# A graph layer on one core: attention in products of 128x128, the message sum in products of 512 columns, one-hots made from SBUF

## What is computed

```python
ea  = edge_attr @ w_e + b_e                       # 131072 x 256
msg = relu(x[src] + ea)
agg = segment_sum(msg, dst, num_segments=8192)
t   = x + agg
h_local = bn(relu(t @ w1 + b1) @ w2 + b2 + x)

hd = x.reshape(256, 32, 256)                      # 256 groups of 32 nodes
q, k, v = split(hd @ in_w.T + in_b)               # 4 heads of 64
attn = softmax(q k^T / 8)                         # 32 x 32 per group and head
h_attn = bn((attn v) @ out_w.T + out_b + x)

out = h_local + h_attn
out = bn(out + relu(out @ m_w1 + m_b1) @ m_w2 + m_b2)
y   = layernorm(x + out)
```

## Time and profile before

| | |
|---|---|
| median of 3 runs | 1954.65 us (1941.84 to 1976.45) |
| the profiled execution | 1932.73 us, its span 1930.9 us |
| TensorE matmul busy | 1567.5 us, 81% |
| TensorE weight load busy | 1182.9 us, 61% |
| VectorE busy | 761.7 us, 39% |
| ScalarE busy | 817.6 us, 42% |
| GpSimd busy | 970.3 us, 50% |
| mean granted clock of TensorE | 0.865 |

### The profile page before, as it was taken

The page is one execution under the profiler, slowest core; times in us unless marked ns, Lnnn a source line. Parts: engine busy times, 40 slices in busy tenths (PEclk is TensorE's granted clock), DMA queues, the critical chain, the costliest instruction groups (busy, mean ns, idle before and its releaser), DMA issues.

```text
span 1930.9 us, 30540 instructions
## 1 busy us (share of the span) xinstructions
PE 1567.5 (81%) x11522; PEld 1182.9 (61%) x11522; DVE 761.7 (39%) x1465; ACT 817.6 (42%) x1729; POOL 970.3 (50%) x1032
## 2 busy tenths in 40 slices
PE   5878888887878888887777887888888787888787
PEld 3556566565656666665666665666666566666566
DVE  4334433343333433433433443433433333433343
ACT  2334434453334444444444443444444444444452
POOL 6554534555445555554455554645555455555430
PEclk6779888898888988888888887989888888888899
DMA  8545533444333434433443433433433334433321
GB/s 292 166 164 178 183 109 99 118 125 121 96 93 113 131 116 118 122 111 93 118 120 110 123 105 104 133 113 113 125 104 114 111 117 114 121 106 107 108 86 34
DMA packets 107385, 233.42 MB, mean 121 GB/s; under 512 B 21731, under 2 KB 46563, under 8 KB 105189
## 3 DMA queue, kind: packets, MB, share of 16 engines
q0 software_dynamic: 49152, 134.28, 24.1%
q1 hardware_dynamic: 56640, 93.87, 14.9%
q10 hardware_dynamic: 1444, 3.30, 0.5%
HBM read 206.20 MB, written 25.17 MB: 120 GB/s over the span
## 4 chain that ended last, share of the span: by engine, by line
PE 66%; issue 15%; another core or an unknown queue 9%; ACT 4%; DVE 4%; DMA 0%; POOL 0%; DVEq 0%; ACTq 0%
PE bank L670 26%; PE bank L716 15%; PE bank L698 14%; PE bank L800 5%; PE bank L786 2%; DVE ml L527 2%; ACT mh L316 2%; PE bank L870 1%; PE bank L704 1%; ACT bank L310 1%; PE bank L725 1%; PE bank L809 1%; ACT h L327 0%; DVE onehot L543 0%
## 5 line engine op out<-in xcount | busy, mean ns | idle before, releaser
L280 POOL DMA_INDIRECT xg<-xb_dram,srcs x864 | 817.2, 946 | 755.5 <-ACT bank L310 520.0
L527 DVE SCALAR_TENSOR_TENSOR ml<-bank,mh 128x512 fp32r<-128x512 f32 x512 | 349.2, 688 | 963.3 <-ACT mh L316 781.4
L316 ACT ACTIVATE mh<-bank 128x512 fp32r<-128x512 f32 x512 | 300.4, 601 | 978.1 <-PE bank L698 551.7
L716 PE MATMUL bank<-mh,onehot 128*128 128x256 f32 x1024 | 346.9, 358 | 123.1 <-DVE ml L527 103.7
L716 PEld LDWEIGHTS bank<-mh,onehot 128*128 128x128 f32 x1024 | 210.7, 206 | 264.5 <-issue 221.6
L310 ACT COPY bank<-xg 128x512 f32<-128x512 f32 x512 | 307.5, 601 | 69.8 <-DVE ml L527 32.8
L698 PE MATMUL bank<-we,ea 64*128 64x256 f32 x2048 | 334.9, 449 | 0.5 <-issue 0.5
L716 PE MATMUL bank<-ml,onehot 128*128 128x256 f32 x1024 | 288.8, 301 | 0.0
L698 PEld LDWEIGHTS bank<-we,ea 64*128 64x128 f32 x2048 | 200.7, 211 | 99.8 <-issue 71.4
L280 POOL DMA_INDIRECT xg<-in_x_dram,srcs x160 | 152.1, 950 | 143.9 <-ACT bank L310 98.8
L716 PEld LDWEIGHTS bank<-ml,onehot 128*128 128x128 f32 x1024 | 215.3, 210 | 1.6
(11 more groups left out here) (100 smaller groups left out, 1319.5 us busy)
## 6 DMA issues: line engine op xcount, KB each, us to landing
ea<-in_ea_dram SPq DMA_DIRECT2D x128, 256.0 KB
xg<-xb_dram,srcs POOLq DMA_INDIRECT x864
xT<-in_xT_dram SPq DMA_DIRECT2D x32, 256.0 KB
aggT<-in_xT_dram SPq DMA_DIRECT2D x32, 256.0 KB
xrow<-in_x_dram SPq DMA_DIRECT2D x8, 1024.0 KB
xb_dram<-xrow SPq DMA_DIRECT2D x8, 1024.0 KB
oT_dram<-oT SPq DMA_DIRECT2D x32, 256.0 KB
xn<-in_x_dram SPq DMA_DIRECT2D x32, 256.0 KB
```

The source lines that it names most:

```text
L280: pool.indirect_dma_start(xg[:, q % NX, n * C:(n + 1) * C], None, t["x"] if q < XB_PAIR else k.xb_dram[:, :], bass.IndirectOffsetOnAxis(k. ...
L316: nc.scalar.activation(mh[:, q % 4, :], EA[q % 3][:, :], ACT.Relu).then_inc(s_mh, 1)
L527: nc.vector.scalar_tensor_tensor(ml[:, q % 4, :], EA[q % 3][:, :], 0.0, mh[:, q % 4, :].bitcast(fp32), ALU.max, ALU.subtract).then_inc(s_m ...
L716: ins = nc.tensor.matmul(G[n % 2][:, 0:C], onehot[:, n % 2, 2 * j + two, :], half[:, q % 4, two * C:(two + 1) * C], start=j == 0 and two = ...
```

## The change

The scores become 8 calls in place of 32 in each iteration: a half of 128 nodes by itself, so that the scores of nodes of different groups are made too and not used. The two banks of the scores become one tensor `both` of 1024 columns, and VectorE reads the four diagonal blocks of 32x32 out of it: maximum, subtraction and the transpose are four instructions each, one per 32 partitions over 8 x 32 elements. `probT` is 128x128 per head with zeros outside the diagonal blocks, set once at the start. The product with v is 8 calls with v as the stationary operand, and its result is already transposed: the copy at p = 14 (L355), the transposes (L809) and their waits are gone, and the copy for the node network moves from p = 16 to p = 14.

`mh` and `ml` become one tile `msg` with high and low side by side; one float32r matmul of 512 columns takes the place of two of 256, and high and low sums arrive in the two halves of the bank `G`. They are added after the group: ScalarE copies the high half to SBUF as before, and VectorE adds the low half onto it (`join_agg`, p = 3, 7, 11, 15) before TensorE's transpose. Since the bank is full, the row of 0 to 127 and the bias row are read from SBUF, and the copies into the bank at the start are gone; the wait for the bias row moves to the first `add_be`.

```diff
-        k.EA, k.G, k.X = k.bank[0:3], k.bank[3:5], k.bank[5:8]
+        k.EA, k.G = k.bank[0:3], k.bank[3:5]
+        k.both = ctx.enter_context(nc.psum_tensor("both", [P, 1024], fp32))
+        k.X = [k.both[:, 0:512], k.bank[5], k.both[:, 512:1024]]
...
-        k.mh, k.ml = sb("mh", [P, 4, 2 * C], f32r), sb("ml", [P, 4, 2 * C], f32r)
+        k.msg = sb("msg", [P, 4, 2, 2 * C], f32r)
...
-                nc.scalar.copy(k.agg[:, :], G[n % 2][:, 0:C]).then_inc(s_agg, 1)
+                nc.scalar.copy(k.agg[:, :], G[n % 2][:, 0:C]).then_inc(s_high, 1)
...
                 if p == 14:
                     act.wait_ge(s_av, i + 1)
-                    if i >= 1:
-                        act.wait_ge(s_oT, i)
-                    nc.scalar.copy(k.on[:, :], X[1][:, :]).then_inc(s_on, 1)
-                if p == PI:
-                    act.wait_ge(s_oT, i + 1)
                     if i >= 2:
...
+            step_of(nc.vector.memset(k.probT[:, :, :], 0.0))
...
                 nc.vector.tensor_tensor(
                     onehot[:, n % 2, :, :],
-                    G[n % 2][:, 2 * P:3 * P].unsqueeze(1).to_broadcast([P, TG, P]),
+                    k.iota[:, :].unsqueeze(1).to_broadcast([P, TG, P]),
...
+            def join_agg(n):
+                dve.wait_ge(s_high, n + 1)
+                nc.vector.tensor_tensor(k.agg[:, :], G[n % 2][:, C:2 * C], k.agg[:, :], ALU.add
+                                        ).then_inc(s_agg, 1)
...
+                quarter = [slice(n * NPG, (n + 1) * NPG) for n in range(P // NPG)]
+                scores = k.both[:, :].rearrange("p (h n) -> p h n", n=P)
...
+                    for g in quarter:
+                        ins = nc.vector.tensor_reduce(k.mx[g, :], scores[g, :, g], AX.X, ALU.max)
...
+                    for g in quarter:
                         ins = nc.vector.tensor_tensor(
+                            k.dif[g, :, :], scores[g, :, g],
+                            k.mx[g, :].unsqueeze(2).to_broadcast([NPG, 2 * H, NPG]), ALU.subtract)
...
+                    for g in quarter:
+                        ins = nc.vector.transpose(k.probT[g, :, g], k.prob[g, :, :])
...
                 for two in range(2):
-                    for half in (mh, ml):
-                        ins = nc.tensor.matmul(G[n % 2][:, 0:C], onehot[:, n % 2, 2 * j + two, :],
-                                               half[:, q % 4, two * C:(two + 1) * C],
+                    ins = nc.tensor.matmul(G[n % 2][:, :], onehot[:, n % 2, 2 * j + two, :],
+                                           msg[:, q % 4, :, two * C:(two + 1) * C],
...
+                            ins = nc.tensor.matmul(X[2 * (h % 2)][:, col:col + P],
+                                                   k.qT[at:at + DH, c, row], k.kT[at:at + DH, c, row],
+                                                   start=True, stop=True)
...
+                            at, col = DH * (h % 2), h // 2 * NB + b * P
+                            ins = nc.tensor.matmul(X[1][at:at + DH, col:col + P],
+                                                   k.vn[:, b, h * DH:(h + 1) * DH],
+                                                   k.probT[:, H * (h % 2) + 2 * b + h // 2, :],
+                                                   start=True, stop=True)
```

More of the change, by code:

```diff
@@ L167, in program @@
         s_out = [sem(f"s_out_stored_{n}") for n in range(2)]
-        s_go = sem("s_general_go")
+        s_go, s_high = sem("s_general_go"), sem("s_high_sum_copied")
         g = General(sem)
@@ L534, in add_be @@
                 dve.wait_ge(s_xrow[m % 2], 16 * (m // 2 + 1))
+                if n == 0:
+                    dve.wait_ge(s_ber, 16)
                 part = k.xrow[:, m % 2, :, half * P:(half + 1) * P]
                 nc.vector.tensor_tensor(
-                    part, G[half][:, 3 * P:4 * P].unsqueeze(1).to_broadcast([P, XB_ROWS, P]), part,
+                    part, k.be_rows[:, half * P:(half + 1) * P].unsqueeze(1).to_broadcast([P, XB_ROWS, P]), part,
                     ALU.add).then_inc(s_xadd, 1)
@@ L647, in _ @@
                     low(slot - 2)
+                if slot % PG == 3 and 1 <= slot // PG <= NG:
+                    join_agg(slot // PG - 1)
                 if slot % PG == 1:
@@ L714, in sum_pair @@
                 for two in range(2):
-                    for half in (mh, ml):
-                        ins = nc.tensor.matmul(G[n % 2][:, 0:C], onehot[:, n % 2, 2 * j + two, :],
-                                               half[:, q % 4, two * C:(two + 1) * C],
-                                               start=j == 0 and two == 0 and half is mh,
-                                               stop=j == PG - 1 and two == 1 and half is ml)
+                    ins = nc.tensor.matmul(G[n % 2][:, :], onehot[:, n % 2, 2 * j + two, :],
+                                           msg[:, q % 4, :, two * C:(two + 1) * C],
+                                           start=j == 0 and two == 0,
+                                           stop=j == PG - 1 and two == 1)
                 ins.then_inc(s_seg, 1)
@@ L780, in attention @@
                     for b in range(2):
+                        row = slice(b * P, (b + 1) * P)
                         for h in range(H):
                             at, c = DH * (h % 2), h // 2
-                            col = (2 * b + c) * NPG
-                            for n in range(4):
-                                o = b * P + n * NPG
-                                ins = nc.tensor.matmul(
-                                    X[2 * (h % 2)][n * NPG:(n + 1) * NPG, col:col + NPG],
-                                    k.qT[at:at + DH, c, o:o + NPG], k.kT[at:at + DH, c, o:o + NPG],
-                                    start=True, stop=True)
+                            col = (2 * b + c) * P
+                            ins = nc.tensor.matmul(X[2 * (h % 2)][:, col:col + P],
+                                                   k.qT[at:at + DH, c, row], k.kT[at:at + DH, c, row],
+                                                   start=True, stop=True)
                     ins.then_inc(s_sc, 1)
@@ L797, in attention @@
                         for h in range(H):
-                            for n in range(4):
-                                r = slice(n * NPG, (n + 1) * NPG)
-                                ins = nc.tensor.matmul(
-                                    X[1][r, b * C + h * DH:b * C + (h + 1) * DH],
-                                    k.probT[r, H * (h % 2) + 2 * b + h // 2, :],
-                                    k.vn[r, b, h * DH:(h + 1) * DH], start=True, stop=True)
-                    ins.then_inc(s_av, 1)
-                if p == 15:
-                    pe.wait_ge(s_on, i + 1)
-                    for c in range(CC):
-                        for b in range(2):
-                            ins = nc.tensor.transpose(
-                                X[1][:, c * NB + b * P:c * NB + (b + 1) * P],
-                                k.on[:, b * C + c * P:b * C + (c + 1) * P], ident[:, :])
-                    ins.then_inc(s_oT, 1)
+                            at, col = DH * (h % 2), h // 2 * NB + b * P
[3 more added lines that the diff above has]
+                                                   start=True, stop=True)
+                    ins.then_inc(s_av, 1)
             def node(j, step):
```

40 lines of the change are left out of this document (8 added, 32 removed).

## The result

| | before | changed |
|---|---|---|
| median of 4 runs each, on one chip | 1950.05 us (1941.84 to 1976.45) | 1787.34 us (1775.59 to 1790.50) |
| ratio, 95% interval | | 0.9167 [0.9102, 0.9233] |
| span of the profiled execution | 1930.9 us | 1783.1 us |
| TensorE busy, idle | 1567.5, 363.4 us | 1446.6, 336.5 us |
| mean granted clock | 0.865 | 0.90 |

What follows compares the result with a forecast made beforehand. TensorE was taken as the bound, its small attention products limited by how fast instructions reach the array. −300 − 93 − 11 + 64 = −340 us on 1930.9 gave 1591, stated as 1600 us; range 1420 to 1720.

Steps and rivals of the forecast that it cites:

- Rival C: TensorE stalls per instruction anywhere, so gaps move and waiting shrinks only to the remaining matmuls' share, 0.63: 1740 us; chance 0.13.
- Attention, −300 us: TensorE's scores, product with v and transposes: 390 us removed, 32 × 2.8 us added for the larger matmuls.
- The clock, −93 us: TensorE's slow clock behind the small products' gaps goes with them: 2.9 us an iteration.
- The sum, −11 us: Message sum on TensorE: two matmuls of 512 columns for four of 256 save 0.022 us a pair.
- rival D: The 512-column float32r message sum runs at float32's pace of two passes: +645 us, so 2240; chance 0.04.
- VectorE on v's path, +64 us: Quarter maxima and subtractions take full-instruction time, so TensorE's v waits for the subtraction: 2.0 us an iteration.
- A: Likeliest rival: terms as summed, TensorE's late-arriving signals staying about one an iteration; range 1540 to 1660; chance 0.53.
- B: TensorE's late-arriving signals, caused by the mass of instructions, go too: −176 us, about 1500 with half kept; chance 0.28.
- One-hots, bias, copies, `join_agg` at zero: SBUF reads, removed copies and VectorE's join cost nothing on the path: one-hot length unchanged, join covered by a slot.

Runs made afterwards that it cites:

- before_no_gathers: The kernel before, with GpSimd gathering only the first 8 pairs and their rows used again, so messages are wrong: 1356.91 us.
- no_gathers: The changed kernel, with GpSimd gathering only the first 8 pairs and their rows used again, so messages are wrong: 1432.72 us.
- sum_only: The kernel before with the changed message sum, `join_agg` and the one-hots from SBUF, attention untouched: 1924.21 us, ratio 1.0112.

## Why the prediction was wrong, step by step

**What bounds the kernel: the reading that failed.** I read "issue" inside the small products as "a limit on how fast instructions reach the array", and let it go with them. `before_no_gathers` has all 4,096 small matmuls and no gap: the 216.8 us of "issue" are 0.0. TensorE was held up from outside, by GpSimd's gathers. This is why "TensorE had 216.8 us of idle removed" and "TensorE's idle time fell by 27 us" are both true: the hold-ups stayed and met other work. Rival C had the direction, a chance of 0.13 and 1740 us, but its formula (waiting shrinks only to the share of matmuls that stay, 0.63) isn't what happened either: idle time went to 0.93 of what it was. A part of the gaps did move, as C says, to the large matmuls of the sum: 57.2 us of "issue" for 19.0, and none in `no_gathers`. That the change is faster at all, which I gave 0.94, came out right for a reason that I didn't have: it removed places where the hold-up showed, and where nothing is held up it is 5% slower.

The Trainium skill had the direction right for the scores. "TensorEngine Tiling (Array Packing)", section "Theoretical Speedup", gives small packed products a speedup of up to 16 times; undisturbed, the packed scores take 0.69 us and the large ones 1.09 (909.41 to 910.50 in `no_gathers`), 1.6 times. The product with v takes 1.03 us packed and 1.02 large (923.54 to 924.56). I had set that rule aside because of the mean of 4.6 us, when the one stretch without a gap showed the price of the operation itself.

**Attention, −300 us.** As bookkeeping it was right: removed 390, added 37.2 + 35.0 = 72 us for a forecast of 90. As a gain it was wrong. Undisturbed, and from start to start, the old parts are 0.69 + 1.03 us and 0.53 for the transposes (638.97 to 639.50 in `before_no_gathers`), 2.25 an iteration, and the new ones 1.09 + 1.02 = 2.11: over 32 iterations the change can save 4 us there, and everything else was the hold-up's.

**The clock, −93 us.** The mean rose to 0.90, not to 0.93. It rises to 0.97 or 0.98 where the gathers hold nothing up, so most of the slow stretches are a consequence of the hold-ups and went only as far as those did.

**The sum, −11 us.** Mis-sized, and its upper bound held: from the first matmul of the sum to the next product it is 0.57 us with four of 256 columns (622.51 to 623.08 above) and 0.57 with two of 512:

```profile
910.50 0.73 PE L712 MATMUL bank<-msg,onehot 128*128 128x512 f32 x2
911.07 1.89 PE L667 MATMUL bank<-o,m 128*128 128x256 f32 x8
```

I had counted 10 ns a matmul beside its columns, which two matmuls fewer should save; at these two places they don't. Nor does a matmul of 512 take float32's two passes: rival D has no ground.

**VectorE on v's path, +64 us.** Right in size and place where nothing else disturbs: a quarter instruction takes 420 ns, as much as a full one, and v waits 1.9 us an iteration, where it waited 2.8 us in all in `before_no_gathers`. That is 57 of the 76 us by which the span of `no_gathers` exceeds that of `before_no_gathers`. Another 16.5 are the price of the wait in clock, which I had left out: the matmuls of v behind it take 82.7 us in place of 66.2, and in one such place, 664.5 to 669.5 behind a wait of 1.71 us, the granted clock is 0.66. Under late signals the wait was 139 us in one execution and 61.5 in another. I treated the late signals as a constant sum beside it. In the case of 542.79 they add up inside it: the change put a chain of signals, TensorE to VectorE to TensorE, on the path, and the first came late. In the other execution they fell on the sum instead.

**Late signals stay (A) or go (B).** They grew, 223.5 to 415.1 us on `high`. B's argument, one cause for gaps and late signals, was true; its conclusion, that both go with the small products, was not, since the products weren't the cause.

**One-hots, bias, copies, `join_agg` at zero.** For `join_agg` borne out within 5 us where nothing is held up; one-hots, bias and copies have no run of their own, and the 57 and 16.5 us above leave little of the 76 for everything else together. With hold-ups `sum_only` is 9 to 34 us slower by its interval; a part of this is not resolved. The one-hot kept its 1216 ns. The contention of which "SBUF — State Buffer", section "Who interferes with whom", of the Trainium skill speaks is there: a gather took 985 ns in the mean for 0.95 us, and 1.69 beside the one-hot of 532.14 above. In the first 800 us of the changed kernel the gathers that overlap a one-hot or an `add_be` take 1.14 us in the mean and the others 0.96; in the kernel before both take 0.95. In the same section the page says that DMA never contends with a compute engine. For the plain transfers the runs agree (1429 and 1432 us, no hold-up); with the indirect ones TensorE, ScalarE and VectorE are held up for some 360 us on the chips that show it, by whatever way, so nothing should be planned on that sentence for them.

## What to carry to other kernels

Idle time called "issue" or "remote" can be a symptom with its cause elsewhere: before a change is priced by removing it, remove the suspected disturber (here the indirect transfers of an engine that the chain never names) and see what the same instructions cost without it. The price of an operation is its undisturbed stretch, not its mean. And a wait with an engine's queue behind it costs its own length, the slow clock behind it (16.5 us here for 57 of waiting), plus the delay of a signal that it hangs on. Doing the work that it waits for first in its slot shortened it at one place, but gained no time that these runs show (1787 us).

## What was not expected of the hardware

- On four chips indirect DMAs from GpSimd hold up TensorE's instructions, its signals and so the clock: 1795 us with them, 1432 with plain transfers of the same bytes from the same queue, 1793 with indirect ones of neighbouring rows. Half as many cost nothing (1435). The late signals end 0.9 to 2.5 us after a row of such DMAs does (64 of 76 in the changed kernel).
- It differs from chip to chip. The same kernel before took 1950 us in the first comparison, 1900, 1892, 1900 and 1894 us on four chips, and 1361 on a fifth. Each of the five ran one group only, so a lasting property of the chip and its state at that time can't be told apart. The sign of the change depends on it: −8% and −5% where there is a hold-up, and +5% (1.0487, with the pacing wait) where there is none.
- A VectorE instruction on 32 partitions takes as long as on 128: 420 ns for 32x256, maximum and subtraction alike.
